# A convolution on row halves of the array, two batches at once, with half of one tile's table-lookup sums moved to GpSimd

## What is computed

```
L0_cond: out = conv1d(x, weight, taps 9, padding 4, groups 4) + (c @ c_weight.T)[:, :, None] + bias
L0_ffn:  w_up, w_down = dequantised 4-bit codes (16-entry table NF4) * absmax
         y1 = x1 @ w_up + b_up + x1 @ lora_a @ lora_b ; x2 = relu(y1)
         y2 = x2 @ w_down + b_down + x2 @ lora_a' @ lora_b'          (1024 -> 2752 -> 1024)
(x is added to the result)
L1_cond: per batch a 64x64 kernel, mixed from 8 by a small perceptron and softmax; out = kernel @ x + bias
L1_ffn:  top-1 of 8 experts, each 1024x1024, chosen by a gate per row
```

## Time and profile before

| what | value |
|---|---|
| median of 3 runs | 1440.43 us (1439.1 to 1441.9) |
| the profiled execution, its own time | 1440.07 us |
| its span in the trace | 1438.6 us |
| TensorE busy (share of span) | 1398.8 us (97%) |
| VectorE, ScalarE, GpSimd busy | 79%, 53%, 15% |
| mean granted TensorE clock | 0.994 |

### The profile page before, as it was taken

One profiled execution on the slowest core, in us unless ns is written; L12 is line 12 of the kernel. 1 busy time (PEld: TensorE's weight loads), 2 busy tenths in 40 slices (PEclk: granted clock), 3 DMA queues, 4 the chain that ended last, 5 costly groups with the idle time before them and its releaser, 6 DMA issues.

```text
span 1438.6 us, 20752 instructions
## 1 busy us (share of the span) xinstructions
PE 1398.8 (97%) x6817; PEld 1146.1 (80%) x6817; DVE 1137.8 (79%) x1101; ACT 755.7 (53%) x839; POOL 211.0 (15%) x218
## 2 busy tenths in 40 slices
PE   7899999999999999999999999999999899999996
PEld 7888888888888888888888888887755688888785
DVE  6869887878877787887878878787644699999895
ACT  5655554545546455464554644643123277777672
POOL 0111000000000000000000000000011266665443
PEclk9999999999999999999999999999999999999998
DMA  6864656568665686656865667756668547969951
GB/s 221 315 223 165 236 209 254 196 250 273 237 246 203 234 292 229 227 218 227 294 240 206 240 220 281 256 191 240 238 231 287 160 121 194 354 190 303 332 146 35
DMA packets 102680, 331.48 MB, mean 230 GB/s; under 512 B 15220, under 2 KB 22908, under 8 KB 102620
## 3 DMA queue, kind: packets, MB, share of 16 engines
q1 hardware_dynamic: 79556, 258.56, 48.4%
q0 software_dynamic: 22816, 71.85, 17.9%
q10 hardware_dynamic: 256, 0.40, 0.1%
HBM read 295.63 MB, written 46.14 MB: 238 GB/s over the span
## 4 chain that ended last, share of the span: by engine, by line
PE 85%; DMA 6%; DVE 3%; issue 2%; ACT 2%; SPq 0%; ACTq 0%; POOL 0%; DVEq 0%; POOLq 0%
PE pair L1133 26%; PE pair L1135 26%; PE pair L1134 25%; PE pair L1187 4%; DMA z_rows<-z 3%; DMA wraw<-exp_w 3%; PE pair L1402 1%; DVE wf L808 1%; PE pair L1214 1%; PE pair L1271 1%; PE pair L1197 1%; ACT z L718 1%; DVE wlr L1108 1%; PE pair L1369 1%; PE pair L1183 1%
## 5 line engine op out<-in xcount | busy, mean ns | idle before, releaser
L808 DVE TENSOR_TENSOR wf<-wf,term 128x1024 f32<-128x1024 f32 x308 | 376.7, 1223 | 65.7 <-ACT term L593 50.5
L593 ACT ACTIVATE term<-codes 128x1024 f32<-128x1024 int32 x308 | 320.6, 1054 | 139.4 <-DVE wf L808 139.4
L1133 PE MATMUL pair<-wh,hh 128*128 128x512 f32 x672 | 263.4, 392 | 3.2 <-DVE ring L871 1.4
L1134 PE MATMUL pair<-wl,hh 128*128 128x512 f32 x672 | 262.0, 390 | 0.0
L1135 PE MATMUL pair<-wh,hl 128*128 128x512 f32 x672 | 262.0, 390 | 0.0
L1133 PE MATMUL pair<-ring,wh 128*128 128x512 f32 x656 | 255.5, 390 | 0.0
L1134 PE MATMUL pair<-ring,wh 128*128 128x512 f32 x656 | 255.3, 389 | 0.0
L1135 PE MATMUL pair<-ring,wl 128*128 128x512 f32 x656 | 255.2, 389 | 0.0
L741 ACT ACTIVATE whr<-wraw 128x1024 fp32r x184 | 187.9, 1055 | 85.3 <-PE pair L1135 50.8
L866 DVE TENSOR_TENSOR acc<-acc,pair 128x1024 f32<-128x1024 f32 x160 | 194.4, 1216 | 47.2 <-PE pair L1135 39.8
L1108 DVE TENSOR_TENSOR wlr<-wraw,whr 128x1024 fp32r<-128x1024 f32 x184 | 213.3, 1215 | 12.5 <-ACT whr L741 12.2
(11 more groups left out here) (178 smaller groups left out, 1527.6 us busy)
## 6 DMA issues: line engine op xcount, KB each, us to landing
ring<-x_parts SPq DMA_DIRECT2D x320, 512.0 KB, 6.4
wraw<-exp_w SPq DMA_DIRECT2D x64, 512.0 KB, 11.2
x_parts<-stage POOLq DMA_DIRECT2D x24, 512.0 KB, 6.0
xg<-exp_b POOLq DMA_DIRECT2D x23, 512.0 KB, 8.0
codes<-codes_up SPq DMA_DIRECT2D x22, 512.0 KB, 5.8
codes<-codes_dn SPq DMA_DIRECT2D x22, 512.0 KB, 5.6
am<-am_dn SPq DMA_DIRECT2D x22, 512.0 KB, 3.7
acc<-x_nat POOLq DMA_DIRECT2D x16, 512.0 KB, 5.5
```

Source lines behind the costliest of these rows:

```text
L593: return nc.scalar.activation(out, codes[:, n % 2], ACT.Relu, scale=scale, bias=-scale * bend)
L808: nc.vector.tensor_tensor(whole(n), whole(n), term[:, e % 2], op).then_inc(term_added, 1)
L1133: mm(ps, ah, bh, start=first, stop=False)
L1134: mm(ps, ah, bl, start=False, stop=False)
```

## The change

`conv(p)` now makes two batches at once. Each matmul uses half of the rows (64 partitions): the lower rows work for one batch while the upper rows work for the other, and in a second turn they swap. The partition order of `xcv` and `tz` is changed to position first, channel second, so that each half of the rows holds four of the eight positions. For one of the two shifts (`part` 0) the table's half is zero in half of its columns, and these are left out: such a matmul has 64 columns of moving data rather than 128. The bias matmuls stand between the two turns, and TensorE waits there for the first turn's end. Two batches are drained by one ScalarE and one VectorE instruction of 1024 columns rather than two each of 512.

The ramps of tiles 1 and 3 go into a double buffer `odd` of their own and are added by GpSimd (`add_odd`), among its DRAM stores. All 24 batches of the first part are now ahead of `up(0, 0)`, and `up(0, 1)` follows it directly.

```
-            for k in range(FIRST):
-                conv(k)
-                if k == 6:
+            for p in range(LATE // 2):
+                conv(p)
+                if p == 7:
                     pe.wait_ge(lora_split, 2)
                     lora_product(0, 0)
-                elif k == 15:
+                elif p == 9:
                     lora_product(0, 1)
             up(0, 0, (0, 2)).then_inc(up_mm, 1)
-            for k in range(FIRST, LATE):
-                conv(k)
             for i in rounds(pe, UNITS // 2):
...
-                wait(pe, x1l_ready, k - 3)
-                whole_bank = bank[4 + k % 4].rearrange("p (j o) -> p j o", j=J)
-                mm(whole_bank, ones[:].bitcast(F32R), ctxd[h][:, k - LATE * h:k - LATE * h + 1].broadcast_to([P, J, CH]),
-                   start=True, stop=False)
-                for g in range(GROUPS):
-                    for d in range(2):
-                        ins = mm(whole_bank[:, :, g * GC:(g + 1) * GC], xcv[h][p % 4][:, k % 2, g, d:d + P], tz[h][:, d, g],
-                                 start=False, stop=g == GROUPS - 1 and d == 1)
-                ins.then_inc(conv_mm, 1)
+                wait(pe, x1l_ready, k - 2)
+                sums = [bank[4 + (k + b) % 4].rearrange("p (j o) -> p j o", j=J) for b in range(2)]
+                for turn in range(2):
+                    for g in range(GROUPS):
+
+                        for part in (1, 0):
+                            for r in range(2):
+                                rows, b, d = slice(r * HP, (r + 1) * HP), r ^ turn, r ^ part
+                                js = slice(0, J) if part else slice(r * J // 2, (r + 1) * J // 2)
+                                ins = mm(sums[b][:, js, g * GC:(g + 1) * GC], xcv[h][p % 4][rows, b, g, d:d + P],
+                                         tz[h][rows, d, g, js.start * GC:js.stop * GC], start=turn == g == 0 and part == 1,
+                                         stop=turn == 1 and part == 0 and g == GROUPS - 1)
+                                if turn == 0 and part == 0 and g == GROUPS - 1:
+                                    ins.then_inc(turn_mm, 1)
+                    if turn == 0:
+                        for b in range(2):
+                            mm(sums[b], ones[:].bitcast(F32R), ctxd[h][:, k + b - LATE * h:k + b + 1 - LATE * h].broadcast_to(
+                                [P, J, CH]), start=False, stop=False)
+
+                        pe.wait_ge(turn_mm, 2 * (p + 1))
+                ins.then_inc(conv_mm, 2)
...
+            def add_odd(n, m):
+                e = NCH * (n // 2) + m - 1
+                pool.wait_ge(odd_ready, e + 1)
+                if m == 1:
+                    pool.wait_ge(head_ready, n + 1)
+                else:
+                    pool.wait_ge(odd_added, e)
+                op = ALU.add if TERMS[m][0] > 0 else ALU.subtract
+                nc.gpsimd.tensor_tensor(whole(n), whole(n), odd_term(e), op).then_inc(odd_added, 1)
...
+            for m in range(1, NCH + 1):
+                add_odd(1, m)
+                if m > 3:
+                    pool.wait_ge(x1l_ready, CB)
+                    store_x1(0, m - 4)
```

More of the change, by code:

```diff
@@ L38 @@
 LATE = 24
-FIRST = 21
+HP = P // 2
 GQ = 32
@@ L154, in program @@
         wh = sb(late, "wh", [P, 2, 4, L], F32R)
+        odd = []
+        for k in range(2):
+            sb(conv, f"first_hidden{k}", [P, L])
+            odd.append(sb(conv, f"odd{k}", [P, L]))
+        conv.close()
         hh = sb(late, "hh", [P, 4, CHUNK], F32R)
@@ L263, in program @@
         am_in = sem("am_in")
+        odd_ready, odd_added, turn_mm = sem("odd_ready"), sem("odd_added"), sem("turn_mm")
         head_ready, term_ready, term_added, scaled, ab_mm, w_ready, wh_ready, wl_ready = (sem(n) for n in (
@@ L354, in _ @@
             load_pair(1)
+            load_codes(0, 1)
             load_pair(2)
@@ L612, in ramps, with odd_ramps, odd_passed @@
                     look(term[:, e % 2], n, m).then_inc(term_ready, 1)
+            def odd_ramps(n, terms):
+                for m in terms:
+                    e = NCH * (n // 2) + m - 1
+                    wait(act, odd_added, e - 1)
+                    look(odd_term(e), n, m).then_inc(odd_ready, 1)
+            def odd_passed(n):
+                act.wait_ge(term_added, NCH * n)
+                act.wait_ge(odd_ready, NCH * (n + 1) // 2)
+                act.sem_inc(term_ready, NCH)
             def lora_high(i, n):
@@ L650, in _ @@
                     lora_high(0, 0)
[L651 to L657, removed]
+                elif p < 7:
+                    ramps(0, 0, ((4,), None, (5,), (6,), (7,))[p - 2])
+                elif p == 7:
+                    lora_high(0, 1)
+                elif p == 8:
                     high(0, 0)
[L659 to L662, removed]
+                elif p == 9:
+                    odd_passed(1)
                     head(0, 2)
-                elif k == 18:
-                    ramps(0, 2, (1,))
-                elif k == 20:
+                elif p == 10:
                     high(0, 1)
+                if 0 < p < NCH + 1:
+                    odd_ramps(1, (p,))
             lora_high(0, 2)
-            ramps(0, 2, range(2, 8))
+            ramps(0, 2, (1,))
+            head(0, 3)
+            odd_ramps(3, (1,))
+            ramps(0, 2, (2, 3))
+            odd_ramps(3, (2,))
+            ramps(0, 2, (4, 5))
+            odd_ramps(3, (3,))
+            ramps(0, 2, (6, 7))
+            relu(0, 0)
+            odd_ramps(3, (4,))
             high(0, 2)
-            relu(0, 0)
-            for k in range(FIRST, LATE):
-                conv_high(k)
-            head(0, 3)
             lora_high(0, 3)
-            ramps(0, 3, range(1, 8))
+            odd_ramps(3, (5, 6, 7))
+            act.wait_ge(odd_added, 2 * NCH)
+            relu(0, 1)
             high(0, 3)
-            relu(0, 1)
-            for k in range(LATE, B):
-                conv_high(k)
+            for p in range(LATE // 2, B // 2):
+                conv_high(p)
+            odd_passed(3)
             for i in rounds(act, UNITS // 2):
@@ L866, in add_down, with conv_low @@
                 nc.vector.tensor_tensor(a, a, pair[2 + j % 2][:], ALU.add).then_inc(acc_added, 1)
[L868 to L878, removed]
+            def conv_low(p):
+                c, col = 2 * p // CB, 2 * p % CB * CH
+                dve.wait_ge(x1h_ready, 2 * p + 2)
+                parts = stages[c][:, :, :, col:col + 2 * CH].rearrange("p j s (b o) -> p s j b o", b=2)
+                nc.vector.tensor_tensor(parts[:, 1], pair[2 + p % 2][:].rearrange("p (b j o) -> p j b o", b=2, j=J),
+                                        parts[:, 0], ALU.subtract).then_inc(x1l_ready, 2)
+            add_ramps(0, 0, (1,))
+            for p in range(LATE // 2):
+                conv_low(p)
+                if p == 0:
+                    add_ramps(0, 0, (2, 3))
+                elif p == 3:
                     dve.wait_ge(lora_split, 1)
@@ L911, in _ @@
             hidden_low(0, 0)
-            for k in range(FIRST, LATE):
-                conv_low(k)
-            add_ramps(0, 3, (1,))
+            low(0, 2)
             lora_low(0, 3)
-            add_ramps(0, 3, range(2, 8))
             scale(0, 3)
             add_lora(0, 3)
+            hidden_low(0, 1)
+            conv_low(LATE // 2)
             low(0, 3)
-            hidden_low(0, 1)
-            for k in range(LATE, B):
-                conv_low(k)
+            for p in range(LATE // 2 + 1, B // 2):
+                conv_low(p)
             for i in rounds(dve, UNITS // 2):
```

112 lines of the change are left out of this document (55 added, 57 removed).

## The result

| what | value |
|---|---|
| changed kernel, median of 4 runs | 1468.41 us (1466.28 to 1469.46) |
| before, 4 runs beside it | 1439.76 us (1437.59 to 1441.9) |
| ratio | 1.0197, 95% interval 1.0177 to 1.0218 |
| predicted | 1452.0 us, range 1436 to 1463 |
| the changed kernel timed twice more (below) | 1460.46 and 1457.89 us, ratios 1.0113 [1.0086, 1.0140] and 1.0115 [1.0084, 1.0146] |

The change makes the kernel slower, as predicted, but in the first timing by more than the range allowed. Its cost is not the same in each timing: the two later medians lie inside the range. The profiled execution took 1469.24 us, with a span of 1467.8.

The account below looks back on a forecast made before the run. TensorE was taken as the bound, the first `down` moving the end one for one: 6.4 + 0.8 + 0.15 + 3.9 + 1.0 - 0.6 = +11.7 us on 1440.4 gave 1452 us, range 1436 to 1463.

Parts of the forecast that it names:

- twelve pairs and the low-rank switches: Convolution ahead of `up(0, 0)`: each pair 0.40 us longer, plus 0.8 for switches around two low-rank products.
- ahead of `up(0, 0)`: Wait from the last batch to the first up product: about 3.8 us instead of 3.67, +0.15.
- between the up products: With no batches between `up(0, 0)` and `up(0, 1)`, TensorE stands still while banks 0 and 1 empty: +3.9 us.
- the up products themselves: `up(0, 0)` and `up(0, 1)`: no added time in the sum; a low clock only as a rival.
- the last four pairs, with the old wait of 0.62: Convolution after the up products: pairs 0.40 us longer each, less 0.6 for a wait that goes.
- ahead of `down`: Wait from the last batch to the first `down`: 2.4 us instead of 1.41, because drains are wider, +1.0.
- The pair: Two batches on TensorE: 4.44 us instead of 4.04, from 3.56 for 32 slots, 0.48 bias and 0.4 switches.
- the second rival: During `up(0, 0)`, VectorE and GpSimd additions block each other: `hidden_low(0, 0)` 3 us late, 1455 us in all; chance 0.2.
- the main case: Whole kernel: the summed terms hold, 1452 us, own range 1447 to 1457; chance 0.55.
- The clock after a stand: Rival: the 3.9 us stand between up products may bring another low clock, 1.6 us, 1453.5; inside the main case.
- GpSimd: Its additions of 1024 columns: about 2.2 us each, tile 1's hidden; value taken 0, range 0 to +4.

Follow-up runs that it names:

- e3: The changed kernel with 16 spare matmuls on TensorE ahead of the first pair; 1456.82 us, ratio 1.0114.
- e7: The kernel before with TensorE's waits filled by spare matmuls, 16 ahead of the first batch and 15 ahead of `up(0, 0)`; 1439.25 us, ratio 0.9981.
- e1: The changed kernel with no zero blocks left out, so every convolution matmul has 128 columns; 1460.44 us, ratio 1.0140.
- e2: The changed kernel with GpSimd's 14 additions cut from 1024 columns to 8; 1461.45 us, ratio 1.0131.
- e9: The changed kernel with both 16 spare matmuls ahead of the first pair and GpSimd's additions cut to 8 columns; 1449.77 us, ratio 1.0048.
- e10: The changed kernel without an edit, timed a third time; 1457.89 us, ratio 1.0115.
- e4: The changed kernel with the old whole-row convolution on TensorE, all else as changed; 1461.47 us, ratio 1.0138.
- e6: The changed kernel with the twelfth pair put between the up products and tile 3's additions ahead of the stores; 1456.03 us, ratio 1.0099.
- e8: The changed kernel without an edit, timed a second time; 1460.46 us, ratio 1.0113.
- e5: The kernel before with only the row-half convolution and its layout, all ramps on VectorE; 1451.51 us, ratio 1.0059.

## Why the prediction was right in sign and wrong in size

The prediction followed one number, the first `down`, and up to there its working can be checked term by term. Measured from the first profile unless another is named:

| term | predicted us | measured us |
|---|---|---|
| twelve pairs and the low-rank switches | 5.6 | 5.0 (e3 against e7, both at full pace) |
| start at the low pace | none | 5.4 |
| ahead of `up(0, 0)` | 0.15 | 0.05 |
| between the up products | 3.9 | 7.6 |
| the up products themselves | none (1.6 as a rival) | 1.9 (0.16 and 1.76) |
| the last four pairs, with the old wait of 0.62 | 1.0 | 0.6 |
| ahead of `down` | 1.0 | 1.1 |
| sum | 11.7 | 21.7, of 21.8 seen |

**Right.** The pair: 4.44 predicted, 4.38 measured, and e1 shows that columns cost nearly nothing. Timeline of PEld, the weight loads of one turn, after:

```profile
37.73 1.87 PEld L1231 LDWEIGHTS pair<-tz,early_xcv 64*128 64x128 f32 x32
```

These 32 loads, 16 on each half of the rows, take 1.87 us: 0.11 us from one to the next in a half, with no gap, as the prediction had it. The Trainium skill, "TensorEngine Tiling (Array Packing)", section "Theoretical Speedup", gives row tiling up to twice the speed; the trace has two halves at work at once and still a slower pair (4.38 us against 4.04), and the measurement decides. Three waits were right to about 0.1 us: 3.72, 2.51, and the stand of 3.78 once GpSimd's additions are out (e2). GpSimd's additions for tile 1 are hidden, as said. And e9, which takes out the two largest costs that the sum lacks, took 1449.8 us, 8.1 above the kernel before. Its first `down` at 117.89 is 10.5 us later than before, near the 11.7 of the sum, but that is partly luck: the sum lacks 1.9 us of low clock in the up products, and e9's spare matmuls save 1.7 us of slow start that the kernel before has too.

**The failed term, between the up products.** "Between the up products [...] TensorE stands still: +3.9" took `hidden_low` to start as soon as ScalarE's `hh` was there. VectorE's seven additions ahead of it took 5.6 us more than in e2, by the blocking that the second rival described. That rival forecast `hidden_low` 3 us late; it is 3.8 late (94.30 instead of 90.5), and e2 gives all of it back. The rival's mechanism should have been in the main case. The Trainium skill, "SBUF — State Buffer", "Who interferes with whom", has it that a VectorE instruction with two SBUF inputs contends with a GpSimd one that reads SBUF, and that one with at most one SBUF input, outside the two-port modes, does not. The trace agrees: L876, with one input in PSUM, takes its usual 1.22 us inside GpSimd's addition of 91.48 to 93.83, while L835 with two in SBUF is stretched to 1.58, from 0.69 in e2.

**The missing term, the start.** The prediction counted sixteen pairs at full pace from 8.6 us on. Before, only the first batch ran at the low pace, to about 12 us, a loss of 1.7 us (45.85 against 44.2 in e7). After, the low pace lasted to 24 us in the first profile, and cost 7.1 us against e3. It differs from run to run: in e10 it ended at 16 us and cost 3.4. The earlier trace rows hid it with a clock of 1.00 from 8.61 us on. The first instructions of PE before, by their durations, show it:

```profile
9.20 3.09 PE L1187 MATMUL pair<-tz,xcv 128*128 128x128 f32 x16
...
12.37 1.95 PE L1187 MATMUL pair<-tz,xcv 128*128 128x128 f32 x16
```

The run e3 shows that the low pace, not the row halves as such, is what is lost there. With halves of 128 columns (e1) and with whole rows (e4) it ended by 12.4 us, in six profiles with 64-column matmuls between 13.7 and 24. One profile each of e1 and e4 is too little to call that the cause; why the start was longer stays open.

**The clock after a stand.** It came, as the rival said: 1.76 us in `up(0, 1)` behind 7.59 us, and also behind 3.78 us (a granted clock of 0.87 in e9). Behind the 1.32 us of e6 it did not: a granted clock of 1.00.

**GpSimd.** 2.2 us estimated, 2.35 measured undisturbed, 2.66 in the mean.

**The rest of 1468.** Beyond the first `down` 7.7 us more were lost in the last stage of the first profile; e10 without them ends at 1454.5, with the first `down` as late as in e8. That the end moves one for one with the first `down` holds as far as the third stage, which comes 956.5 to 958.6 us later in all twelve profiles. It fails behind that: from there to the first expert product it is 82.1 to 87.4 us, and the last stage takes 286.7 to 299.0, neither with a relation to the first `down`. Whether the change makes the late load more frequent can't be told from three profiles.

**What the parts cost.** By the medians, row halves alone 0.6% (e5), all of it 1.1% (e8, e10), 2.0% in the first timing. So by its three medians the change costs between 16 and 29 us, and the first `down`, 20 to 22 us later in its three profiles, tells more than any one median here.

## What to carry to other kernels

Before columns of moving data are saved, find what paces the matmuls: where each instruction still loaded 128 weight columns, narrower moving data saved next to nothing (0.05 us a pair), and splitting the rows cost 0.34 us a pair. Work given to GpSimd wasn't free for VectorE where both read two SBUF operands: count the length of each such addition in VectorE's queue, and see whether something short and urgent stands behind it. A batch of other work between two products that share banks is cover for the drain; when it was moved here, the drain and the low clock after it appeared.

## What was not expected of the hardware

- TensorE's matmuls had the lengths of the low level (32 row-half instructions in 3.68 us, later 2.00) for up to 15 us, while the granted clock in the windows read 1.00. With 16 spare matmuls ahead the first pair had full pace.
- After a stand of 3.67 us filled with 15 spare matmuls, `up(0, 0)` ran at full pace from its first instruction; with the stand it lost 1.6 us.
- One load of the last stage arrived late in some executions of the same kernel and not in others: TensorE waited 5.5 us for it in both of two, and 1.3 at most in the third.
